# A fused four-layer attention and gated-FFN kernel: softmax context moved by DMA and divided in pairs instead of being transposed

## The reference

```python
xn = _layernorm(x, axis=-1)
s = attention(xn)               # 32 heads of 16; output projection at its end
g = _silu(ffn(xn))
x = x + s * g                   # x is [4, 256, 512] f32
# inside attention:
scores = einsum('bhsd,bhtd->bhst', q, k) / sqrt(16)
attn = softmax(scores)          # causal in layers 0, 2, 3; full in layer 1
ctx = einsum('bhst,bhtd->bhsd', attn, v).transpose(0, 2, 1, 3).reshape(b, s, 512)
return ctx @ Wo
```

## Time and profile before

| | |
|---|---|
| median of 3 runs | 1331.58 us (1330.56 to 1336.55) |
| profiled execution, its own time | 1332.45 us |
| its span in the trace | 1330.7 us |
| attention run 0 (slots) | about 188 to 635 us |
| FFN of layer 2 | about 635 to 880 us |
| attention run 1 (slots) | about 885 to 1267 us |

### The profile page before, as it was taken

The page is one execution under the profiler, slowest core; times in us unless marked ns, Lnnn a source line. Parts: engine busy times, 40 slices in busy tenths (PEclk is TensorE's granted clock), DMA queues, the critical chain, the costliest instruction groups (busy, mean ns, idle before and its releaser), DMA issues.

```text
span 1330.7 us, 22702 instructions
## 1 busy us (share of the span) xinstructions
PE 1216.5 (91%) x8860; PEld 900.0 (68%) x8860; DVE 808.3 (61%) x1322; ACT 652.6 (49%) x1106; POOL 385.9 (29%) x460
## 2 busy tenths in 40 slices
PE   4999999999999999979999999999899889898897
PEld 3788876666656556546777787776666666676664
DVE  8743467665675645674655566536776776765444
ACT  3333357555454555554333333336665655565653
POOL 1000125333210101021344434405532342424443
PEclk9999989999999999979999999899999999999999
DMA  6000000110000100001242222120001001000001
GB/s 254 0 1 0 1 34 3 48 58 2 1 2 2 36 1 1 26 25 48 72 142 95 95 72 80 64 80 3 2 2 40 2 2 34 1 25 23 2 1 63
DMA packets 15259, 48.07 MB, mean 36 GB/s; under 512 B 2858, under 2 KB 6959, under 8 KB 14388
## 3 DMA queue, kind: packets, MB, share of 16 engines
q1 hardware_dynamic: 15156, 46.63, 10.1%
HBM read 44.00 MB, written 2.10 MB: 35 GB/s over the span
## 4 chain that ended last, share of the span: by engine, by line
PE 71%; DVE 14%; ACT 8%; issue 4%; DMA 2%; POOL 0%; POOLq 0%; DVEq 0%; ACTq 0%; SPq 0%
PE bank L650 18%; PE bank L766 14%; PE bank L680 8%; PE bank L909 8%; PE bank L869 6%; PE bank L817 4%; PE bank L783 3%; DVE negmax L1816 3%; ACT probs L1381 3%; PE bank L849 2%; ACT pv L1389 2%; PE bank L880 2%; DMA W_lo_whole<-in_w 2%; PE bank L797 1%; PE bank L826 1%
## 5 line engine op out<-in xcount | busy, mean ns | idle before, releaser
L1816 DVE TENSOR_REDUCE negmax<-bank 128x4 f32<-128x1024 f32 (+1 forms) x256 | 250.3, 1017 | 77.0 <-PE bank L826 66.2
L1381 ACT ACTIVATE probs<-bank 128x1024 f32<-128x1024 f32 (+1 forms) x256 | 218.0, 865 | 46.0 <-PE bank L849 37.7
L2023 POOL TENSOR_SCALAR_AFFINE_SELECT probs<-probs 128x512 f32<-128x512 f32 x192 | 125.9, 666 | 292.3 <-ACT probs L1381 292.1
L1966 POOL TENSOR_TENSOR W_lo<-W_lo_whole,W_hi 128x1536 fp32r<-128x1536 f32 x28 | 98.4, 3516 | 155.8 <-ACT W_hi L1132 155.8
L817 PE MATMUL bank<-kT,qT 64*128 64x256 f32 (+1 forms) x1024 | 110.5, 312 | 30.1 <-DVE negmaxT L1834 8.8
L817 PEld LDWEIGHTS bank<-kT,qT 64*128 64x128 f32 x1024 | 81.4, 191 | 65.9 <-issue 33.2
L869 PE MATMUL bank<-probs,V 128*32 128x256 f32 (+1 forms) x2048 | 119.6, 352 | 6.6 <-DVE negmax L1816 5.1
L1389 ACT ACTIVATE pv<-bank 128x256 f32<-128x256 f32 x128 | 49.2, 384 | 154.1 <-PE bank L869 153.6
L849 PE MATMUL bank<-qT,kT 64*128 64x256 f32 (+1 forms) x640 | 113.4, 384 | 3.7 <-DVE h_lo_whole L1638 1.6
L1132 ACT ACTIVATE W_hi<-W_lo_whole 128x1536 fp32r<-128x1536 f32 x28 | 41.7, 1488 | 130.6 <-DVE W_lo_whole L1592 130.6
L650 PE MATMUL bank<-xT_hi,W_hi 128*128 128x512 f32 x224 | 91.7, 410 | 5.6 <-ACT silu L1145 4.5
(11 more groups left out here) (205 smaller groups left out, 2692.3 us busy)
## 6 DMA issues: line engine op xcount, KB each, us to landing
W_lo_whole<-in_w SPq DMA_DIRECT2D x28, 768.0 KB, 4.1
Wqkv_lo_whole<-in_Wqkv SPq DMA_DIRECT2D x6, 768.0 KB, 6.7
Wo_lo_whole<-in_Wo SPq DMA_DIRECT2D x4, 1024.0 KB, 4.9
Wqkv<-in_Wqkv SPq DMA_DIRECT2D x2, 1536.0 KB, 7.5
Wdown_whole<-in_Wd SPq DMA_DIRECT2D x1, 2816.0 KB, 14.6
x<-in_x SPq DMA_DIRECT2D x4, 512.0 KB, 5.4
out<-x SPq DMA_DIRECT2D x8, 256.0 KB, 2.0
V_lo_whole<-in_V SPq DMA_DIRECT2D x1, 1408.0 KB, 5.8
```

The lines of the kernel that those rows point to most:

```text
L1381: nc.scalar.activation(A[l].probs[gi % 2][kb][:, :, q0 - kb * A[l].probs1:].rearrange("p (b h) q -> p b h q", b=2), B.tensor(key)[:, :, 0: ...
L1816: v.tensor_reduce(A[l].negmax[u % 2][:, qb, :].rearrange("p (b h) -> p b h", b=2)[:, :, 2 * g:2 * g + 2], B.tensor(key)[:, :, 0:2 * nk].re ...
L1966: gp.tensor_tensor(lo, whole, hi.bitcast(F32), ALU.subtract).then_inc(w_low.sem, 1)
L2023: gp.affine_select(out=blk, in_=blk, compare_op=ALU.is_ge, fill=0.0, base=0, pattern=[[0, 4], [1, P]], channel_multiplier=-1).then_inc(cau ...
```

## The change

The two transposes are taken out. After `take_pv` the SP queue issues five small DMAs per group (`move_values`): four move each head's 16 context rows to 16 of 64 partitions of `parts`, and the fifth reads the four rows of sums and writes each 16 times to `sums`. Two groups, a pair, fill 128 partitions. In every even slot from 4 on DVE takes the reciprocal of the pair's `sums` (128x256, in place) and multiplies it with `parts` into one of six slots of a ring; heads lie on partitions already, as `project_out` wants them. In GQA layers ACT rounds the pair (`context_high`, 128x256) at the end of the slot after, behind `take_pv`, and GpSimd forms the rest (`context_low`). `weigh_values` uses bank 6 in place of 4 or 7, and in slots with an output product goes ahead of it. The SP queue's order is now by slots. `residual` writes its product over `gate`; the splitting of layer 3's output weights is spread over three slots of U = 10 and no longer over four. In `ffn2` the last pair's `context` stands behind `hidden`.

```diff
-def context_bank(r, U):
-    return 6 if U < RUN - 1 else (5, 4)[r]
-def values_bank(l, U, g):
-    return 7 if not GQA[l] and g % 2 == 0 and U + 1 + g // 2 < RUN else 4
+def values_bank(U, g):
+    return 6 if U + 2 + g % 2 < RUN else 4
...
+def pair_scaled(G):
+    return (G - 4) // 2 if G >= 4 and G % 2 == 0 else None
+def pair_split(G):
+    U, g = divmod(G, GROUPS)
+    if U == RUN - 2 and g >= 2:
+        return pair_scaled(G)
+    return pair_scaled(G - 1)
...
+        def moved(r, G):
+            return pv_moved[G % 2], 16 * MOVES * ((RUN * GROUPS * r + G) // 2 + 1)
...
@@ TensorE: turn_context and turn_rows are gone
-                pe.wait_ge(*B.emptied(("ctxT", l, b, tau)))
+                pe.wait_ge(*(ctx_low if GQA[l] else ctx_scaled).at(l, 4 * (b + 1)))
...
                 if G >= 1 and not filled_out:
                     weigh_values(r, G - 1, G)
-                if G >= 2:
-                    turn_context(r, G - 2, G)
...
-                for n in rows_turned(r, U, g):
-                    turn_rows(*n, OUT_BANK[n[2]])
-                for n in rows_projected(r, U, g):
+                projected = rows_projected(r, U, g)
+                if projected and filled_out:
+                    weigh_values(r, G - 1, G)
+                for n in projected:
                     project_out(*n, 1 if U % 2 == 1 else (4, 5)[n[2]])
...
-                if G >= 1 and filled_out:
+                if G >= 1 and filled_out and not projected:
                     weigh_values(r, G - 1, G)
...
@@ ScalarE: take_pv, take_rows, slot
+                if G >= 2:
+                    act.wait_ge(*moved(r, G - 2))
                 nc.scalar.activation(A[l].pv[gi % 2][:], B.tensor(key)[:, 0:SEQ], copy).then_inc(B.empties(key), 1)
-            def take_rows(l, b, tau):
...
+            def context_high(r, q):
+                l, qi = pair(r, q)
+                if GQA[l]:
+                    act.wait_ge(*ctx_scaled.at(l, qi + 1))
+                    nc.scalar.activation(ctx_hi[r][:, q % RING, :], ctx_whole[r][:, q % RING, :], copy).then_inc(ctx_high.sem, 1)
...
-                for n in rows_turned(r, U, g):
-                    take_rows(*n)
...
                 if G >= 1:
                     take_pv(r, G - 1)
+                if pair_split(G) is not None:
+                    context_high(r, pair_split(G))
...
@@ VectorE: ffn2
-                context(0, last)
                 scale_weights(CHUNKS2_EARLY + 1)
                 hidden(2, CHUNKS2_EARLY)
+                context(0, last)
                 scale_weights(CHUNKS2_EARLY + 2)
...
@@ VectorE: context takes a pair, context_low is gone
+            def context(r, q):
+                l, qi = pair(r, q)
+                dve.wait_ge(*moved(r, 2 * q))
+                dve.wait_ge(*moved(r, 2 * q + 1))
+                sums = A[l].sums[q % 2][:]
+                v.reciprocal(sums, sums).then_inc(rs_ready.sem, 1)
+                if q >= RING:
+                    ll, qq = pair(r, q - RING)
+                    dve.wait_ge(*B.filled(("O", ll, qq // 4, 1)))
+                dve.wait_ge(*rs_ready.at(l, qi + 1))
+                v.tensor_tensor(ctx_whole[r][:, q % RING, :], A[l].parts[q % 2][:], sums, ALU.mult).then_inc(ctx_scaled.sem, 1)
...
-                if G >= 2:
-                    context(r, G - 2)
+                if pair_scaled(G) is not None:
+                    context(r, pair_scaled(G))
...
-                for n in rows_turned(r, U, g):
-                    if GQA[n[0]]:
-                        context_low(*n)
...
@@ GpSimd: context_low
+            def context_low(r, q):
+                l, qi = pair(r, q)
+                if GQA[l]:
+                    pool.wait_ge(*ctx_high.at(l, qi + 1))
+                    gp.tensor_tensor(ctx_lo[r][:, q % RING, :], ctx_whole[r][:, q % RING, :],
+                                     ctx_hi[r][:, q % RING, :].bitcast(F32), ALU.subtract).then_inc(ctx_low.sem, 1)
...
+                if pair_split(G) is not None:
+                    context_low(r, pair_split(G))
...
@@ SyncE: the five moves, and the queue's order by slots
+            def move_values(r, G):
+                l, gi = group(r, G)
+                q = G // 2
+                sp.wait_ge(*B.emptied(("PV", l, gi)))
+                if q >= 2:
+                    ll, qq = pair(r, q - 2)
+                    sp.wait_ge(*ctx_scaled.at(ll, qq + 1))
+                pv, row, first = A[l].pv[gi % 2], SEQ, 64 * (G % 2)
+                for i in range(4):
+                    load(A[l].parts[q % 2][first + HD * i:first + HD * (i + 1), :], pv[32 * i:32 * i + HD, :], pv_moved[G % 2])
+                load(A[l].sums[q % 2][first:first + 64, :], bass.AP(pv, HD * row, [[32 * row, 4], [0, HD], [1, SEQ]]), pv_moved[G % 2])
...
+            def slot(r, G):
+                U, g = divmod(G, GROUPS)
+                if g == 2 and U + 1 < RUN:
+                    place_maxima(r, U + 1)
+                if r == 0 and g == 3:
+                    loads_0(U + 1)
...
+                if G >= 1:
+                    move_values(r, G - 1)
+                if r == 1 and g == 3:
+                    loads_1(U + 1)
```

More of the change, by code:

```diff
@@ L51 @@
 CELL = HD + 4
+RING = 6
+MOVES = 5
 NEG = -1.0e30
@@ L433, in program @@
         assert at[0] <= R + 102496
-        at = [R + first["ctxT_lo"]]
+        at = [names["ctxT0_hi"][0]]
         tanh1 = [place(f"tanh1_{i}", [P, D], F32, at) for i in range(2)]
@@ L503, in program @@
         m_rows = [sem(f"max_rows_placed{i}") for i in range(2)]
+        pv_moved = [sem(f"weighed_values_moved{i}") for i in range(2)]
         out_done = sem("output_stored")
@@ L872, in weigh_values @@
                 ins.then_inc(B.fills(key), 1)
[L874 to L885, removed]
-                pe.wait_ge(*B.emptied(("ctx", l, 8 * b + 7)))
-                for c in range(KC):
-                    ins = nc.tensor.transpose(ps[:, c * P:(c + 1) * P], A[l].ctxr[b % 2][:, tau, c * P:(c + 1) * P], ident[:])
-                ins.then_inc(B.fills(key), 1)
             def project_out(l, b, tau, bank):
@@ L1068, in ffn3 @@
                     if e == CHUNKS3_EARLY:
-                        turn_context(1, last - 1, last)
                         weigh_values(1, last, last)
-                    if e == CHUNKS3_EARLY + 1:
-                        turn_context(1, last, last)
-                        for tau in range(2):
-                            turn_rows(3, SEQS - 1, tau, 6 + tau)
-                    if e == CHUNKS3_EARLY + 2:
+                    if e == CHUNKS3_EARLY + 3:
                         for tau in range(2):
@@ L1259, in ffn2 @@
                 gate_silu(2, CHUNKS2_EARLY)
-                for tau in range(2):
-                    take_rows(1, SEQS - 1, tau)
                 weights_high(CHUNKS2_EARLY + 1)
@@ L1306, in ffn3 @@
                     if e == CHUNKS3_EARLY + 1:
-                        for tau in range(2):
-                            take_rows(3, SEQS - 1, tau)
+                        context_high(1, RUN * GROUPS // 2 - 2)
+                    if e == CHUNKS3_EARLY + 2:
+                        context_high(1, RUN * GROUPS // 2 - 1)
                         bias2_high()
@@ L1435, in slot @@
                     take_pv(r, G - 1)
+                if pair_split(G) is not None:
+                    context_high(r, pair_split(G))
                 if r == 1 and U == 2:
                     wqkv_high_part(3, g)
-                if r == 1 and U == 10:
-                    wo_high_part(3, g)
+                if r == 1:
+                    for c in WO3_SLOTS.get((U, g), ()):
+                        wo_high_part(3, c)
                 if r == 1 and (U, g) in SPLIT3_SLOTS:
@@ L1760, in ffn3 @@
             def ffn3():
-                last = RUN * GROUPS - 1
+                last = RUN * GROUPS // 2 - 1
                 for e in range(CHUNKS3_EARLY, 2 * HC3):
@@ L1768, in ffn3 @@
                         context(1, last)
-                        for tau in range(2):
-                            context_low(3, SEQS - 1, tau)
-                    if e == CHUNKS3_EARLY + 2:
+                    if e == CHUNKS3_EARLY + 3:
                         for tau in range(2):
@@ L2037, in slot @@
                     wqkv_low_part(3, g)
-                if r == 1 and U == 10:
-                    wo_low_part(3, g)
+                if r == 1:
+                    for c in WO3_SLOTS.get((U, g), ()):
+                        wo_low_part(3, c)
                 if r == 1 and (U, g) in SPLIT3_SLOTS:
@@ L2133, in place_maxima, with loads_0 @@
                          m_rows[u % 2])
-            for hh in range(2):
-                load(Wqkv_whole[0][hh][:], a["Wqkv0"][:, :, hh, :], qkv_in[0][hh])
-            sp.wait_ge(*B.filled(("out", 0, TILES - 1)))
-            load(Wo_whole[0][:], a["Wo0"], wo_in)
-            for U in range(RUN):
-                place_maxima(0, U)
+            def move_values(r, G):
[9 more added lines that the diff above has]
```

(2 more changed lines are left out.)

150 lines of the change are left out of this document (70 added, 80 removed).

## The result

The changed kernel takes 1364.9 us in the median (1361.93 to 1370.83, 4 runs); the kernel before takes 1332.74 us beside it (1330.56 to 1336.55, 4 runs). The ratio is 1.0244 [1.0197, 1.029], so the change costs about 32 us. The forecast was 1343.5 us, or +11.9 us: slower, as it came out, within the range, but with little over a third of the size.

A forecast was written before the change was run, and what follows sets the result against it. PE (91% busy) was taken to bound the kernel, except g = 2 slots ending on or near DVE's maxima. Gains of 34.7 us against added 6.2 + 8.4 + 7 + 3 + 16.8 + 5.2 gave +11.9 us: 1343.5 us, range 1314 to 1368.

The forecast's parts named there:

- The reciprocal: DVE's reciprocal of 128x256 context sums, 64 in all: taken as 2.0 us each, with ends 0.4 and 2.0 us.
- The wait that it makes: After g = 2 slots PE's plain scores wait for DVE's maxima; 1.23 us later in 5 slots without row transposes or products.
- The idle time at the last products of layer 1: Sign that the forecast is right: PE idle about 6 us at the last output products of layer 1.
- SP's issues: Five context moves on the SP queue, 0.65 us each to issue; no cost as long as an issue stays under 0.9 us.
- the rival of the SP queue: SP's issues set the pace from 0.9 us on: 38 us more, 1382 us; chance 0.14 together with other late arrivals.
- Step (a): Context transposes removed from PE: 0.22 us a slot, 14.1 us gained in 64 odd slots, 4.4 us in g = 0.
- (d): DVE's division ahead of the maxima in g = 2 slots: +6.2, +8.4 and +7 us, plus 3 us of rotary work slipping.
- the streaming reciprocal: Rival: DVE's reciprocal streams at 0.4 us, so g = 2 slots mostly end on PE again; 1317 us, chance 0.16.
- (c): Value matmuls ahead of output products on PE cover the products' 9.9 us of waits for plain-score maxima: 9 us gained.
- (e): ACT rounds 48 pairs between value copy and next exponential, without slack there: 0.35 us each, +16.8 us.
- (g): Five moves per group on the SP queue, 3.3 us in slots of 4.2 to 9 us, land in time: nothing added.
- (f): FFN of layer 2: DVE's last division delays the output products, +5.2 us; layer 3's last products, one chunk back, 0.

## Why the prediction was right in sign and short in size

**Right.** The reciprocal: 1743 ns for 256 elements, 6.8 ns an element, inside the 5.4 to 7.3 that the slope between one and eight elements gave, while the streaming cast of that size takes 0.4 us. By the prediction's estimate from the Trainium skill (VectorE: DVE Perf Modes, "First, the fixed hardware budget") it would have been 2.1 us and a start; the runs say 1.74, and the measurement decides. The wait that it makes: 1.78 us at the plain scores, where the slot was to grow by 1.23 us (it grew by 1.34). The idle time at the last products of layer 1, 6.14 us. SP's issues, 0.60 us each, below the point from which SP would set the pace; DVE waited 8.1 us for moves in all, so the rival of the SP queue falls. Step (a): the first value matmul starts 0.27 us behind the last projection matmul, as in the slots without transposes.

**Mis-sized: the price of the division (d).** In the prediction, the streaming reciprocal was some 26 us cheaper than the slow one. Measured, the copy is 61 us cheaper. The waits for the maxima were not far off: (d) had 6.2 + 8.4 + 7 = 21.6 us for them, and they grew by 27.8 (8.8 to 36.6 us). Two things were left out. The first is the other places where something waits for DVE: beside the maxima and the FFN of layer 2 the prediction gave them 3 us, and in the kernel with the places mended the length alone still costs 32, with hardly a change in the wait for the maxima. The second is the clock: I priced PE's work behind a wait at its old durations, and behind 10 of the 25 waits the granted clock fell, in the slot shown for over 6 us of PE's work. The estimate gives the clock 12 to 14 us of the whole loss, and its exact share stays open.

**Wrong: the values ahead of the output products (c).** Forecast -9 us; measured +5.5 in the kernel before, and 9 us in the kernel with the maxima first. The reading was wrong to begin with: of the 9.9 us in the earlier trace rows only 5.3 end with the maxima, and those went down to 2.6. And the step put the value matmuls ahead of the product in every slot that has one, where residual, maxima and plain scores follow the product. I counted that delay only as 0.58 us in 12 slots, 7 us under (d), so that the two together came to -2 us.

**Not borne out: ScalarE's rounding (e).** Forecast +16.8 us, as 0.35 us in 48 slots. In the slot at 206 us the exponential does start 0.93 us after the first scores, where it was 0.60, but that slot is an exception: the usual delay is 0.12 us, in 24 slots, some 3 us. What failed is the claim that ScalarE has no slack there: most of the 0.41 us of a rounding fits in. Another order is worth nothing in the changed kernel and some 9 us once the maxima are out of the way. What the rounding costs by being there at all wasn't run.

**Wrong: nothing for SP's order (g), and nothing at the end of layer 3 (f).** I asked whether the moves land in time and not what stands behind them: the chunk's load stood some 5 us behind them. With the load a slot earlier that unit was 1.8 us shorter, and no gain of the whole is shown. The ends of layer 3 lose about 4.5 us to the chain of move, division, rounding and subtraction, which one chunk doesn't cover.

That the forecast fell within its range owes something to luck, for the errors partly offset. With (e) at 3 us (13.8 less), the values' order at the +5.5 us of its own run where (c) and its delay had -2 (7.5 more), and the reciprocal at the copy's 61 us (35 more), the sum comes to some 40 us, 8 more than the 32 measured. The single prices don't add, as the values' order shows once more in the mended kernel, and this remainder isn't settled.

## What to carry to other kernels

Before putting a long operation on an engine, list what the tensor engine waits for on that engine, and put the short, awaited step first: here that order alone was worth 28 us. Then ask at every other place that waits for this engine what the longer step does there: with the order mended, its length still cost 32 us. Price a new wait of PE with the clock that may fall behind it, by rows of the same matmul at both levels, and not by its own length alone. And when a change frees one queue, reckon the ends of the stages one by one, since there is no repeated saving there to pay for the new work.

## What the runs showed of the hardware that was not expected

- Behind a wait of PE of 1.78 us the granted clock went from 1.00 to 0.50 and stayed there from 212.28 to past 218 us, with PE busy 100% of that stretch. Four matmuls of one shape took 0.69 us instead of 0.34. The clock fell so behind 10 of PE's 25 waits for the maxima, and behind one of 14 in the kernel before (a wait of 3.13 us). Across the whole kernel, PE's busy time for the same 8476 matmuls is 25 us less with all the orders mended than in the changed kernel.
- A multiplication of 256 elements with both operands in SBUF took 3.52 us (0.43 us elsewhere) beside a subtraction of 3.42 us on GpSimd, ending 0.3 us after it; a subtraction of 512 elements took 3.49 us (0.71 us in the median) beside another of GpSimd's. In the kernel before the multiplication read one operand from PSUM. The Trainium skill (SBUF — State Buffer, "SBUF: two separate sides") calls the pair of ports that these two engines share an exclusive lock, held for a whole instruction, when the VectorE operation has two SBUF inputs; this case's rows agree.
- A reciprocal of 128x256 fp32 takes 1743 ns, 6.8 ns an element, and a copy of the same tile 373 ns, 1.5 ns an element.
- The last move to land at the end of layer 3, 64 KB within SBUF, took 2.99 us from the end of its issue to the release of its reader.
